# A conditioned residual product: how the last group's first store is cut

## The reference

```python
def reference(x, itok_B_0_15, L0_cond_weights):
    W = weights[condition]                       # (64, 128, 128): one matrix for each batch
    return x + jnp.einsum('bct,bcd->bdt', x, W)
```

## Time and profile before

| what | us |
|---|---|
| median of three runs | 320.37 |
| lowest, highest | 320.07, 320.59 |
| the profiled execution | 320.04 |
| its span in the trace | 318.3 |
| last store issued | 310.25 |

### The profile page before, as it was taken

How to read it: one execution, slowest core, us unless ns; L and a number is a source line. 1 busy time by engine, 2 the same in 40 slices (tenths; PEclk the granted TensorE clock), 3 DMA queues, 4 the chain that set the end, 5 groups by cost and what they waited for, 6 DMA issues and landing times.

```text
span 318.3 us, 1351 instructions
## 1 busy us (share of the span) xinstructions
PE 246.5 (77%) x512; PEld 104.6 (33%) x512; DVE 146.8 (46%) x65; POOL 18.9 (6%) x69
## 2 busy tenths in 40 slices
PE   0099999991996979779398895939979596796960
PEld 0044444440442424334143342414424242342420
DVE  0026766762252553735237362641626556055460
POOL 0000000000010000001000010000000001000000
PEclk9999999998796998999779799996979999598996
DMA  8999999999999999999999999999999999999997
GB/s 329 416 441 457 371 424 457 397 461 399 457 424 432 449 408 461 412 445 432 424 453 404 457 424 432 445 412 461 399 457 424 432 449 408 461 395 461 420 411 298
DMA packets 5187, 135.29 MB, mean 425 GB/s; under 512 B 578, under 2 KB 578, under 8 KB 578
## 3 DMA queue, kind: packets, MB, share of 16 engines
q1 hardware_dynamic: 2448, 68.16, 50.0%
q10 hardware_dynamic: 2738, 67.11, 48.9%
HBM read 68.16 MB, written 67.11 MB: 425 GB/s over the span
## 4 chain that ended last, share of the span: by engine, by line
DMA 61%; PE 33%; DVE 3%; issue 0%; SPq 0%
PE product L92 33%; DMA out<-x_ring 32%; DMA x_ring<-x 30%; DVE x_ring L108 3%; SPq L58 0%
## 5 line engine op out<-in xcount | busy, mean ns | idle before, releaser
L92 PE MATMUL product<-x_ring,chosen_weights 128*128 128x512 f32 x512 | 246.5, 644 | 61.4 <-DMA x_ring<-x 61.4
L108 DVE TENSOR_TENSOR x_ring<-product,x_ring 128x2048 f32<-128x2048 f32 x64 | 146.7, 2291 | 161.4 <-PE product L92 161.4
L92 PEld LDWEIGHTS product<-x_ring,chosen_weights 128*128 128x128 f32 x512 | 104.6, 207 | 202.4 <-issue 122.7
L80 POOL COPY chosen_weights<-weight_table 128x128 f32 x64 | 18.7, 293 | 284.6 <-DVE x_ring L108 277.7
L102 DVE TENSOR_SCALAR state_row<-condition_row 1x64 int32<-1x64 int32 x1 | 0.2, 182 | 2.0 <-DMA condition_row<-condition 2.0
L137 POOL MEMSET const-float32-0.0<- 128x1 f32 x1 | 0.1, 98 | 0.1
L137 POOL MEMSET const-bfloat16-1.0<- 128x1 bf16 x1 | 0.1, 101 | 0.0
L137 POOL MEMSET const-uint8-127<- 128x1 uint8 x1 | 0.1, 101 | 0.0
L137 POOL MEMSET const-float32-1.0<- 128x1 f32 x1 | 0.1, 98 | 0.0
L137 POOL BASE_LOAD x1 | 0.0, 12 | 0.1
## 6 DMA issues: line engine op xcount, KB each, us to landing
x_ring<-x SPq DMA_DIRECT2D x16, 4096.0 KB, 26.7
out<-x_ring ACTq DMA_DIRECT2D x15, 4096.0 KB, 31.3
out<-x_ring ACTq DMA_DIRECT2D x4, 1024.0 KB, 9.1
weight_table<-weights SPq DMA_DIRECT2D x1, 1024.0 KB, 4.9
condition_row<-condition ACTq DMA_DIRECT2D x1, 0.2 KB
```

The costliest lines, as they stand in the source:

```text
L80: pool.tensor_copy(chosen_weights[b][:, :], weight_table[:, bass.ds(state[b] * features, features)]).then_inc(weights_chosen[b], 1)
L92: last = pe.matmul(product[:, b % psum_slots, m * BANK_COLUMNS:(m + 1) * BANK_COLUMNS], chosen_weights[b][:, :], x_ring[:, bass.ds(b * tim ...
L108: dve.tensor_tensor(tile, product[:, b % psum_slots, :], tile, AluOpType.add).then_inc(sum_done[b], 1)
```

## The change

The store of batch 60 is cut into five transfers. The first moves channels 0 to 111, all of the batch's 2048 columns. The last 16 channels, 112 to 127, follow as four transfers of four channels each: 112 to 115, 116 to 119, 120 to 123 and 124 to 127. All wait for the same sum, `sum_done[12]`, stand in ACT's queue in this order ahead of the wait for batch 61's sum, and raise the semaphore of room 3. The stores of batches 61 to 63 keep their 128 channels. The last wait for room 3 counts four transfers more: 16 x (4 + 3 + 4) = 176 in place of 16 x (4 + 3) = 112.

```diff
             g = groups - 1
+
+            room = g % ROOMS
+            few, parts = 4, 4
             for i in range(GROUP):
-                b = (g % ROOMS) * GROUP + i
-                column = (g % ROOMS) * group_columns + i * time
+                b = room * GROUP + i
+                column = room * group_columns + i * time
                 act.wait_ge(sum_done[b], sums_wanted(g // ROOMS, b))
-                act.dma_start(out[g, :, i * time:(i + 1) * time], x_ring[:, column:column + time]
-                              ).then_inc(room_stored[g % ROOMS], 16)
-            for r in range(ROOMS):
-                act.wait_ge(room_stored[r], 16 * (groups // ROOMS + (GROUP - 1 if r == g % ROOMS else 0)))
+                rows = channels - (few * parts if i == 0 else 0)
+                act.dma_start(out[g, 0:rows, i * time:(i + 1) * time],
+                              x_ring[0:rows, column:column + time]).then_inc(room_stored[room], 16)
+                for row in range(rows, channels, few):
+                    act.dma_start(out[g, row:row + few, i * time:(i + 1) * time],
+                                  x_ring[row:row + few, column:column + time]
+                                  ).then_inc(room_stored[room], 16)
+            for r in range(ROOMS - 1):
+                act.wait_ge(room_stored[r], 16 * (groups // ROOMS))
+            act.wait_ge(room_stored[room], 16 * (groups // ROOMS + GROUP - 1 + parts))
```

## The result

| | before | after |
|---|---|---|
| median of 16 runs, us | 320.12 | 320.81 |
| lowest, highest of them | 319.87, 321.5 | 320.09, 322.5 |
| the profiled execution, its span | 320.04, 318.3 | 320.81, 319.1 |

The ratio is 1.0022, with a 95% interval of 1.0012 to 1.0031: the change costs 0.7 us, just above what a measurement of this kernel can tell from no change. The forecast was 323.7 us, +3.3 us; the sign was right, the size nearly five times too large. The time lies in the stated range.

A forecast was written before the change was run, and what follows sets the result against it. The DMA engines bound the tail, its end the last to empty its queue. Last packet 316.0 - 0.31 + 5.0 = 320.7 against 317.4, +3.3 us; 320.37 + 3.3 = 323.7 us, range 319.8 to 324.9.

The forecast's parts named there:

- The DMA engines bound the tail, and two late ones its end: Tail: queued stores outlast the last sum; 14 engines are done at about 316.0, two at about 317.4 us.
- ACT's four issues are hidden: ACT's queue after batch 60's store: four issues of 0.338 us end at 301.6, before batch 61's sum at 303.39; cost 0.
- The sign that I had named for dearer issues: ACT's queue: batch 61's store issued after 303.5 would mean the issues were dearer than 0.34 us.
- Four rows go to four engines, and the row per engine is worth 0.31 us: Batch 60's store: each small transfer puts one row on four engines; seven rows per engine for eight gain 0.31 us.
- rival B: Tail: a late engine is among the four carrying the small transfers and ends at 317.4 + 0.92; 321.3 us, chance 0.10.
- Four adjacent rows come at one engine's rate, all four engines in step: 5.0 us for four: Small transfers: four engines share one engine's rate, 5.0 us for four rows, last packet 320.7 against 317.4, +3.3 us.
- rival C: Small transfers: adjacent partitions feed two engines, or the four follow each other; +0.7 us, 321.1 us, chance 0.05.
- The 112 rows straddle the sets, with up to 2.2 us, but stay under the rest: 112-row part: rows across two engines' sets wait up to 2.2 us, partly overlapped on the four, elsewhere under +3.3.
- D: Small transfers: rate fully shared with a fifth engine, 6.2 us for four rows; +4.5 us, 324.9 us; 0.52 together with the forecast.
- slower has 0.64: Whole kernel: chance 0.64 of measuring slower by more than 0.64 us, beside same 0.33 and faster 0.03.

The follow-up runs named there:

- the last group of runs: Six kernels cutting batch 60's store otherwise, most with small transfers' rows four or eight apart, against the kernel before: ratios 1.0065, 1.005, 1.0041, 1.0038, 1.002, 1.0052.
- two of 64: Batch 60's store in two transfers of 64 adjacent channels, against the kernel before: ratio 1.0056, +1.8 us by the median.
- eight of 16: Batch 60's store in eight transfers of 16 adjacent channels, against the kernel before: ratio 1.0026, +0.9 us by the median.

## Why the prediction was right or wrong

- *The DMA engines bound the tail, and two late ones its end.* Right: the chain ends with a sum as before, at 310.6 (310.2 in the kernel before; the 0.34 us stand already ahead of the change), and the time moved with the engines' queues alone. The packets of the kernel before show every engine at 9.82 to 9.84 us for the last four stores, and two that start them over a microsecond behind.
- *ACT's four issues are hidden.* Right, though each took 0.46 us in place of 0.34. The sign that I had named for dearer issues would have misled: batch 61's store went out at 303.73, after 303.5, but only because its sum ended at 303.70. With twice as many issues it no longer holds, as the last group of runs shows.
- *Four rows go to four engines, and the row per engine is worth 0.31 us.* Right: 16 small packets more, and ten engines at 9.52.
- *Neither late engine is among the four (against rival B).* Right by the packets.
- *Four adjacent rows come at one engine's rate, all four engines in step: 5.0 us for four.* This is the term that failed. In the changed kernel the four rows took 1.24 us on two of the engines, 1.75 and 2.0 us on the others. Added alone they took at most 2.4 us on the worst engine and 1.24 on two, +0.8 us on the time. That is the size of rival C, the engines following one another (7 x 0.31 = 2.2 us, +0.7 us), to which I gave 0.05. I reckoned with equal shares at every moment. The packets show two engines that lose nothing beside two that lose much, so the four did not wait in step. Stretches of sharing must not be added up as if the sharers stayed together.
- *The 112 rows straddle the sets, with up to 2.2 us, but stay under the rest.* The mechanism was named and then set aside as hidden. It was the other half of the loss: alone it costs +0.9 us with less to move. Once the 5.0 us had shrunk, it was a late engine, slowed in its seven rows, that ended last. An engine with no slack was in that list, and its exposure should have been summed for itself.
- The two halves are 0.9 and 0.8 us alone and 0.7 to 1.0 together: they fall on different engines, and only the last one counts.
- That the sign came out right is in part luck: I had it from the four engines, and a late engine, on which I had counted a row won, ended last.
- Nowhere did I count that the cut could slow rows outside batch 60's store. A late engine's last 32 KB row of group 14's store did take 0.42 and 0.53 us longer, in the changed kernel run again and in the one with 112 channels alone.
- The chances don't add as written: the forecast, D, B and C make 0.67, where slower has 0.64.

The Trainium skill (SBUF — State Buffer, section Door 1: The DMA port swizzle) gives a range of partitions as many times 27 GB/s as it has ports. Its direction holds: adjacent partitions read together are slower, four apart not. Its size for a steady transfer would give, as an estimate, +2.4 us for two of 64 and +7 us for eight of 16; measured were +1.8 and +0.9. Whether adjacent partitions together give one engine's rate, asked for by engines that are not in step, or somewhat more, these runs don't tell. Nor do they tell why in each execution a few engines wait and their partners do not. Shown is, for the small transfers, that the cost lies in which partitions are read together; for the 112 rows, that it is not the place written and that rows of such a store hinder each other. That they do so by straddling is argued, not shown.

## What to carry to other kernels

Before moving a row between DMA engines, ask how the new shape deals partitions to engines: here every other cut of the 128-row transfer cost 0.6 to 2.4 us where the gain in view was 0.3. Read share and rate together: a share of 1.0 with a lower rate was engines in each other's way, a lower share, here, was an issue queue that came late. And where a maximum over engines sets the end, sum each exposed engine by itself, the one without slack first.

## What the runs showed of the hardware

- Four engines that read four adjacent partitions at one time slowed each other (rows up to 0.58 us longer than 0.31); with the same number of rows four apart no row was slow.
- A few engines lose all of it: in the 112-row store alone, twelve engines lost nothing and one lost 1.85 us in seven rows.
- A 32 KB row of a 128-row store, still under way on a late engine while the others read the 112-row part, took 1.66 and 1.77 us in place of 1.25.
- The loss differs from one execution to the next. Run again, the changed kernel's times spread over 2.6 us (320.3 to 322.9) where the kernel before has 1.1 (319.9 to 321.0); in the first comparison it was 2.4 against 1.6.
- Transfers of 16 rows eight apart took 0.62 us to issue where one of 128 adjacent rows took 0.34, and after six of them an issue took 2.4 us.
- By the completions of the stores in the kernel before, one engine lags more with each group, by about 0.1 us. Another stays 1.0 us or more behind the other fourteen from the store of group 1 on, which ends at 71 us; group 0's store, over at 54.6 us, doesn't show it. Between the two the only packet of the instruction queue in the span ran (16 KB, at 62.8 us; in the changed kernel at 55.7, after group 0's store as well). That this packet is the cause is not shown.
